# Attention by seven products: the fifth product's two sums move from ScalarE and GpSimd to VectorE

## The chip, the core and the metric

The kernel runs on one core of a Trainium2 chip. The metric is the device time of one launch in microseconds. Five compute queues run side by side and meet only at semaphores: TensorE (PE in the profile, its weight loads PEld), VectorE (DVE), ScalarE (ACT), GpSimd (POOL), and SyncE (SP), which issues DMAs. The granted TensorE clock is 1.00 of full speed over the whole profiled execution.

## The reference

The reference is a two-layer block on x of 64 x 32 x 512 in fp32: an S4D convolution, attention with 32 heads of width 128, a LoRA projection, an octonion feed-forward network, and a second layer of adapters, a small attention and a mixture of experts. Only the attention of the first layer bears on this change. Cut to what matters, with x of 2048 tokens x 512:

```python
q = x @ wq            # 512 -> 32 heads x 128
k, v = x @ wk, x @ wv
s = q @ k.T * 192 ** -0.5          # inside each batch of 32 tokens, causal
p = softmax(s)
x = x + (p @ v) @ wo               # summed over the 32 heads
```

## The kernel before

**Products.** Every projection is a product of a 2 x 2 block matrix of weights with a 2 x 2 block matrix of activations, and is made by seven products in place of eight (Winograd's form). A *set* is one such product: its seven results are P1 to P7, each 128 x 512 in one PSUM bank, and four outputs are sums of them:

- u2 = P6 + P1
- first output: P2 + P1
- u3 = P7 + u2
- second output: P4 + u3
- third output: u3 + P5
- u2 = u2 + P5, and then the fourth output: P3 + u2

Each fp32 product is made from a high and a low part of both operands by three matmuls (`mm3`, L215 to L217). So a product is 6 matmuls of 512 columns, or in the sets for the values (V) 12 of 256 columns.

**Loops.** `attention` runs 16 iterations: 8 groups of four heads (QUADS) for the first half of the tokens (pair 0), then 8 for the second (pair 1). Iterations 1 to 6 and 9 to 14 are hardware loops; 0, 7, 8 and 15 are written out. An iteration has six sets: 0 and 1 (weights H0, H1), 2 and 3 (values, weights V), 4 and 5 (H2, H3). After sets 0, 1, 4 and 5 come `scores` (16 matmuls of Q with K), a softmax on VectorE (`soft_shift`, `exps` on ScalarE, `soft_divide`, `soft_turn`), `prob_times_v`, and four `output` products with their `add_out`. In pair 0 VectorE also makes the activations' sums for the second half (`part`), which ScalarE stores to HBM by DMA.

**Who frees the banks.** The products use PSUM banks 0 to 2 in rotation (`product_bank`), in the order in which TensorE makes them: P1 of a set (ahead of P4 and P3 of the set before), P6, P5, P2, P7, the next P1, P4, P3. So a product waits until the one three places earlier has been read. Readers before the change: ScalarE copies P1 (`keep_p1`, L1230) and P5 (`keep_p5`, L1237) to SBUF; VectorE's `mix` (L1374, its addition is L1387) reads P6, P2, P7, P4 and P3 from PSUM with one operand in SBUF; GpSimd's `mix` (L1177) adds the copy of P5 to u3 (L1181) and to u2 (L1182). `mix_done` counts VectorE's sums, 5 a set, and `c22_done` GpSimd's.

**Weights.** SyncE loads them to `raw`. For every kind (H0, H1, V, H2, H3) ScalarE makes seven high parts (`high`, L973) and GpSimd seven low parts (`low`, L1007) and four sums of blocks (`sums`, L986, L989, L992, L996). A slot is overwritten once the product that used it is done: `sums` starts when product number 2 (P5) of the set that uses the slots is done, and the high part j waits for product j. A product waits for its own low part by the count in `lo_done`; the parts are made in the order 0 to 6, which is P1, P6, P5, P2, P7, P4, P3.

**Order.** Each queue's order is written out by hand in its `body`. `scores` of a set waits until P3's sum of that set is done, since it reads Q and K, and for the softmax step before (`soft_step`).

Of the kernel before, what the change touches and what calls it, by code (L numbers as in the profile page):

```python
# [14 lines left out]
F32 = mybir.dt.float32  # L15
# [881 lines left out]
PROD_AT = (1, 4, 5, 6, 7, 9, 10)  # L897
# [142 lines left out]
def attention(nc, t, sb, sem, overlaid, const, consts, mm3, resid, psum, kept_raw, kept, hw, v_tok, combos, later):  # L1040
# [7 lines left out]
    with ctx:  # L1048
# [4 lines left out]
        p5 = kept_raw[:, 7 * 2 * VCOLS + TT:7 * 2 * VCOLS + 2 * TT]  # L1053
# [15 lines left out]
        p1_done, p5_done = sem(ctx, "p1_done"), sem(ctx, "p5_done")  # L1069
        mix_done, c22_done = sem(ctx, "mix_done"), sem(ctx, "c22_done")  # L1070
# [56 lines left out]
        def _(sp):  # L1127
# [6 lines left out]
            def load_y(it, j):  # L1134
                sp.wait_ge(prod_done, product_count(it * SETS + SETS - 1, j))
                sp.wait_ge(part_out, 16 * (it * 7 + PART_ORDER.index(j) + 1))
                if j >= 2:
                    sp.wait_ge(y_in[j % 2], 16 * (j // 2))
                sp.dma_start(yc[:, j].bitcast(F32), y_parts[j]).then_inc(y_in[j % 2], 16)
# [31 lines left out]
        def _(pool):  # L1171
# [5 lines left out]
            def mix(it, s):  # L1177
                g = it * SETS + s
                pool.wait_ge(p5_done, g + 1)
                pool.wait_ge(mix_done, mix_count(g, 2))  # L1180
                pool.tensor_tensor(destination(s, 1, 1), u3[:], p5, ALU.add).then_inc(c22_done, 1)  # L1181
                pool.tensor_tensor(u2[:], u2[:], p5, ALU.add).then_inc(c22_done, 1)  # L1182

            def body(it, pair, first=False, turn=False, turned=False, last=False):
                hw.first_low(pool, it, "H1")
                mix(it, 0)
# [4 lines left out]
                mix(it, 1)  # L1191
                hw.last_low(pool, it, "V", fresh=first)
                hw.first_low(pool, it, "H2")
                mix(it, 2)
                hw.last_low(pool, it, "H2")
                mix(it, 3)
                out_low(it * 2 + 1)
                hw.first_low(pool, it, "H3")
                mix(it, 4)
# [3 lines left out]
                mix(it, 5)  # L1203
# [21 lines left out]
        def _(act):  # L1225
# [4 lines left out]
            def keep_p1(it, s):  # L1230
                g = it * SETS + s
                act.wait_ge(prod_done, product_count(g, 0))
                act.wait_ge(mix_done, g * 5 + 2)
                act.activation(p1, psum[:, product_bank(s, 0), :], ACT.Copy).then_inc(p1_done, 1)  # L1234

            def keep_p5(it, s, first=False):
                g = it * SETS + s  # L1237
                act.wait_ge(prod_done, product_count(g, 2))
                if not (first and s == 0):
                    act.wait_ge(c22_done, g * 2)  # L1240
                act.activation(p5, psum[:, product_bank(s, 2), :], ACT.Copy).then_inc(p5_done, 1)  # L1241
# [23 lines left out]
            def body(it, pair, first=False, turn=False, turned=False, last=False):  # L1265
# [6 lines left out]
                keep_p5(it, 0, first)  # L1272
# [9 lines left out]
                keep_p5(it, 1)  # L1282
# [10 lines left out]
                keep_p5(it, 2)  # L1293
# [6 lines left out]
                keep_p5(it, 3)  # L1300
# [5 lines left out]
                keep_p5(it, 4)  # L1306
# [11 lines left out]
                keep_p5(it, 5)  # L1318
# [29 lines left out]
        def _(dve):  # L1348
# [25 lines left out]
            def mix(it, s, k):  # L1374
                g = it * SETS + s
                j = (1, 3, 4, 5, 6)[k]
                dve.wait_ge(prod_done, product_count(g, j))
                out, other = ((u2[:], p1), (destination(s, 0, 0), p1), (u3[:], u2[:]),
                              (destination(s, 1, 0), u3[:]), (destination(s, 0, 1), u2[:]))[k]
                if k == 0:  # L1380
                    dve.wait_ge(p1_done, g + 1)
                    dve.wait_ge(mix_done, g * 5 + 5)
                if k in (2, 3):
                    dve.wait_ge(mix_done, mix_count(g, 0 if k == 2 else 2))
                if k == 4:
                    dve.wait_ge(c22_done, g * 2 + 2)
                dve.tensor_tensor(out, psum[:, product_bank(s, j), :], other, ALU.add).then_inc(mix_done, 1)  # L1387
# [51 lines left out]
            def body(it, pair, first=False, turn=False, turned=False, last=False):  # L1439
# [1552 lines left out]
```

## Time and profile before

| | us |
|---|---|
| median of 3 runs | 2131.43 (2130.31 to 2131.95) |
| profiled execution, its own time | 2132.61 |
| its span | 2130.8 |
| PE busy | 2101.4 (99%), 11928 matmuls |
| DVE busy | 1387.7 (65%) |
| POOL busy | 1248.8 (59%) |
| ACT busy | 718.4 (34%) |

The attention lies from about 89 to 1613 us of the span. Its loop iterations take about 94.5 us each. A matmul of 512 columns shows 390 ns, but the next one starts 0.23 us after it: they are pipelined and their ends are modelled. So a wait of TensorE shows as idle time only by what it exceeds that overlap. In the rows, kept_f is the memory that holds the copies of P1 and P5, wh and kept hold the weights, yc the activations, u is u2 or u3, sc and ex are the softmax's, probT the turned probabilities, v_tok and qk the outputs of the sets.

### The profile page before, as it was taken

What the parts mean: (1) busy time and instruction counts of PE and PEld (TensorE: products, weight loads), DVE (VectorE), ACT (ScalarE), POOL (GpSimd) and SP (SyncE); (2) the same over time, 40 slices, a digit from 0 to 9 for tenths busy, and PEclk for the clock granted to TensorE, in tenths of its full rate; (3) what the DMA queues carried; (4) which work ended last, traced back from release to release, by engine and by line L of the source; (5) the groups of instructions that cost most, each with busy time, mean ns of one, the idle gap of its engine ahead of it and who ended that gap; (6) DMA issues with size and microseconds to landing.
All of it is one profiled execution on the core that took longest, in us unless ns stands there. A gap on an engine that the chain in (4) does not pass through costs nothing. (4 is left out here: it accounts for less than half of the span.)

```text
span 2130.8 us, 36899 instructions
## 1 busy us (share of the span) xinstructions
PE 2101.4 (99%) x11928; PEld 1820.1 (85%) x11928; DVE 1387.7 (65%) x2625; ACT 718.4 (34%) x1444; POOL 1248.8 (59%) x1309
## 2 busy tenths in 40 slices
PE   7999999999999999999999999999999999999999
PEld 6788888989888898989888898989887788878887
DVE  8767777676767767665656566565657766655444
ACT  5333232332323232332323233232323744443332
POOL 3678585777757676776758576776745642114220
PEclk9999999999999999999999999999999999999999
DMA  7421212211111226211111211111112200001110
GB/s 241 154 60 48 55 49 79 54 52 47 49 52 44 75 58 215 61 41 41 40 39 42 67 49 39 39 39 39 40 61 77 90 20 0 0 1 40 39 39 20
DMA packets 122615, 122.28 MB, mean 57 GB/s; under 512 B 35249, under 2 KB 101457, under 8 KB 120497
## 3 DMA queue, kind: packets, MB, share of 16 engines
q1 hardware_dynamic: 91697, 109.87, 16.6%
q10 hardware_dynamic: 29568, 7.34, 1.7%
q0 software_dynamic: 1280, 4.20, 0.7%
q8 instruction: 37, 0.61, 0.1%
q14 instruction: 33, 0.27, 0.0%
HBM read 108.13 MB, written 13.28 MB: 57 GB/s over the span
## 5 line engine op out<-in xcount | busy, mean ns | idle before, releaser
L215 PE MATMUL psum<-yc,wh 128*128 128x512 f32 x904 | 361.4, 400 | 1.4 <-ACT kept_f L1234 0.8
L216 PE MATMUL psum<-yc,wh 128*128 128x512 f32 x904 | 352.9, 390 | 0.0
L217 PE MATMUL psum<-yc,wh 128*128 128x512 f32 x904 | 352.8, 390 | 0.0
L1437 DVE TENSOR_TENSOR resid<-psum,resid 128x512 f32<-128x512 f32 x248 | 171.3, 691 | 138.1 <-PE psum L217 133.8
L215 PE MATMUL psum<-kept,yc 128*128 128x256 f32 x896 | 256.7, 287 | 3.4 <-DVE u L1387 1.6
L217 PE MATMUL psum<-kept,yc 128*128 128x256 f32 x896 | 253.9, 283 | 0.0
L216 PE MATMUL psum<-kept,yc 128*128 128x256 f32 x896 | 253.8, 283 | 0.0
L1007 POOL TENSOR_TENSOR wh<-wh_f,wh 128x256 fp32r<-128x256 f32 x256 | 189.2, 750 | 105.1 <-ACT wh L973 102.9
L1007 POOL TENSOR_TENSOR wh<-raw,wh 128x256 fp32r<-128x256 f32 x192 | 142.0, 740 | 111.7 <-ACT wh L973 111.7
L217 PEld LDWEIGHTS psum<-yc,wh 128*128 128x128 f32 x904 | 169.8, 188 | 36.0
L215 PEld LDWEIGHTS psum<-yc,wh 128*128 128x128 f32 x904 | 170.4, 188 | 33.5 <-issue 1.4
L216 PEld LDWEIGHTS psum<-yc,wh 128*128 128x128 f32 x904 | 170.3, 188 | 30.8
L215 PE MATMUL psum<-o_hi,wo 128*128 128x512 f32 x496 | 194.4, 392 | 0.9 <-DVE resid L1437 0.9
L216 PE MATMUL psum<-o_lo,wo 128*128 128x512 f32 x496 | 194.2, 391 | 0.0
L217 PE MATMUL psum<-o_hi,wo 128*128 128x512 f32 x496 | 193.2, 390 | 0.0
L215 PEld LDWEIGHTS psum<-kept,yc 128*128 128x128 f32 x896 | 171.5, 191 | 8.8 <-DVE u L1387 2.5
L216 PEld LDWEIGHTS psum<-kept,yc 128*128 128x128 f32 x896 | 171.7, 192 | 3.6
L217 PEld LDWEIGHTS psum<-kept,yc 128*128 128x128 f32 x896 | 171.6, 192 | 0.0
L973 ACT ACTIVATE wh<-wh_f 128x256 fp32r<-128x256 f32 x256 | 98.4, 408 | 176.8 <-POOL wh_f L996 158.9
L1241 ACT ACTIVATE kept_f<-psum 128x512 f32<-128x512 f32 x96 | 57.4, 598 | 263.0 <-PE psum L217 263.0
L1234 ACT ACTIVATE kept_f<-psum 128x512 f32<-128x512 f32 x96 | 57.1, 595 | 220.8 <-PE psum L217 204.4
L1387 DVE TENSOR_TENSOR u<-psum,kept_f 128x512 f32<-128x512 f32 x96 | 66.4, 692 | 94.9 <-PE psum L217 93.8
(363 smaller groups left out, 4925.3 us busy)
## 6 DMA issues: line engine op xcount, KB each, us to landing
raw<-in_attn_w SPq DMA_DIRECT2D x96, 512.0 KB, 5.1
wo_f<-in_attn_w SPq DMA_DIRECT2D x31, 512.0 KB, 4.0
hankel<-kernel_rows SPq DMA_DIRECT2D x32, 256.0 KB, 4.6
y_parts<-stage ACTq DMA_DIRECT2D x56, 128.0 KB, 2.3
yc<-y_parts SPq DMA_DIRECT2D x7, 1024.0 KB, 5.1
resid<-in_xT SPq DMA_DIRECT2D x4, 1024.0 KB, 9.7
outT<-wide SPq DMA_DIRECT2D x16, 256.0 KB, 2.6
kept_f<-in_l_w SPq DMA_DIRECT2D x3, 1024.0 KB, 5.5
```

Of the source, the lines that this page charges most:

```text
L215: pe.matmul(out, w[0], x[0], start=start, stop=False)
L216: pe.matmul(out, w[0], x[1], start=False, stop=False)
L217: return pe.matmul(out, w[1], x[0], start=False, stop=stop)
L973: act.activation(self.part(kind, j, 0), src, ACT.Copy).then_inc(self.hi_done, 1)
L1007: pool.tensor_tensor(self.part(kind, j, 1), src, self.part(kind, j, 0).bitcast(F32), ALU.subtract).then_inc(self.lo_done, 1)
L1234: act.activation(p1, psum[:, product_bank(s, 0), :], ACT.Copy).then_inc(p1_done, 1)
L1241: act.activation(p5, psum[:, product_bank(s, 2), :], ACT.Copy).then_inc(p5_done, 1)
L1387: dve.tensor_tensor(out, psum[:, product_bank(s, j), :], other, ALU.add).then_inc(mix_done, 1)
L1437: dve.tensor_tensor(part, psum[:, 5 + (GH + m) % 3, :], part, ALU.add).then_inc(tail_free, 1)
```

## The change

In place of the copy on ScalarE and the two sums on GpSimd, VectorE's `mix` reads P5 from PSUM twice: third output = P5 + u3, then u2 = P5 + u2. That is seven VectorE sums a set, all counted by `mix_done`. `keep_p5`, GpSimd's `mix`, the buffer p5 and the semaphores p5_done and c22_done are gone. TensorE makes P7 ahead of P5: P6, P7, P5, P2, the next P1, P4, P3, and the banks follow. `mix` takes the sums in the order P6, P7, P5 to the third output, P5 to u2, P2, P4, P3. The order of the low and high parts of the weights and the numbers of the products are unchanged (P5 is still number 2, P7 number 4). The places of `scores`, `prob_times_v`, `output`, `add_out`, `part` and the softmax steps are set anew around the sums. The activations that pair 1 loads back come in the new order (Y_ORDER). `keep_p1` now waits for P2's sum of the set before.

```diff
-PROD_AT = (1, 4, 5, 6, 7, 9, 10)
+PROD_AT = (1, 4, 6, 7, 5, 9, 10)
 def product_bank(s, j):
-    return (s * 7 + (-3, 0, 1, 2, 3, 5, 6)[j]) % 3
+    return (s * 7 + (-3, 0, 2, 3, 1, 5, 6)[j]) % 3
 def mix_count(g, k):
-    return g * 5 + (6 + k)
+    return g * 7 + (8 + k)
...
-            def mix(it, s):
-                g = it * SETS + s
-                pool.wait_ge(p5_done, g + 1)
-                pool.wait_ge(mix_done, mix_count(g, 2))
-                pool.tensor_tensor(destination(s, 1, 1), u3[:], p5, ALU.add).then_inc(c22_done, 1)
-                pool.tensor_tensor(u2[:], u2[:], p5, ALU.add).then_inc(c22_done, 1)
...
-                act.wait_ge(mix_done, g * 5 + 2)
+                act.wait_ge(mix_done, mix_count(g, 4) - 7)
                 act.activation(p1, psum[:, product_bank(s, 0), :], ACT.Copy).then_inc(p1_done, 1)
-            def keep_p5(it, s, first=False):
-                ...
-                act.activation(p5, psum[:, product_bank(s, 2), :], ACT.Copy).then_inc(p5_done, 1)
...
+            def mix(it, s, *ks):
                 g = it * SETS + s
+                for k in ks:
+                    name = ("P6", "P7", "P5", "P5", "P2", "P4", "P3")[k]
+                    out, other = ((u2[:], p1), (u3[:], u2[:]), (destination(s, 1, 1), u3[:]), (u2[:], u2[:]),
+                                  (destination(s, 0, 0), p1), (destination(s, 1, 0), u3[:]), (destination(s, 0, 1), u2[:]))[k]
+                    dve.wait_ge(prod_done, product_count(g, PROD[name]))
+                    if k == 0:
+                        dve.wait_ge(p1_done, g + 1)
+                        dve.wait_ge(mix_done, mix_count(g, 6) - 7)
+                    elif k in (1, 2, 6):
+                        dve.wait_ge(mix_done, mix_count(g, {1: 0, 2: 1, 6: 3}[k]))
+                    dve.tensor_tensor(out, psum[:, product_bank(s, PROD[name]), :], other, ALU.add).then_inc(mix_done, 1)
...
                 if not first:
                     soft_shift(sm)
-                mix(it, 0, 1)
+                mix(it, 0, 1, 2, 3, 4)
                 if not first:
                     soft_divide(sm)
-                mix(it, 0, 2)
-                if not first:
                     soft_turn(sm, 1, it * 8)
-                mix(it, 0, 3)
-                mix(it, 0, 4)
+                mix(it, 0, 5, 6)
...
                 elif name != "P1":
-                    pe.wait_ge(mix_done, {"P5": g * 5 + 4, "P2": g * 5 + 5, "P7": mix_count(g, 0),
-                                          "P4": mix_count(g, 1), "P3": mix_count(g, 2)}[name])
+                    pe.wait_ge(mix_done, {"P7": mix_count(g, 5) - 7, "P5": mix_count(g, 6) - 7, "P2": mix_count(g, 0),
+                                          "P4": mix_count(g, 3), "P3": mix_count(g, 4)}[name])
                 elif not start:
-                    pe.wait_ge(p5_done, g)
+                    pe.wait_ge(mix_done, mix_count(g, 1) - 7)
...
                 pe.wait_ge(soft_step, sm * NSOFT - 4)
-                pe.wait_ge(mix_done, mix_count(g, 4))
+                pe.wait_ge(mix_done, mix_count(g, 6))
```

The first place is VectorE in set 0 of an iteration, from the last step of `soft_shift` to the P3 sum of the set (kept_f32 is P1's copy; here a written-out iteration). Before:

```order
L1410 TENSOR_TENSOR sc<-sc,stat 128x256
L1387 TENSOR_TENSOR qk<-psum,kept_f32 128x512
L1417 TENSOR_REDUCE stat<-ex 128x8
L1418 RECIPROCAL stat<-stat 128x8
L1419 TENSOR_TENSOR ex<-ex,stat 128x256
L1387 TENSOR_TENSOR u3<-psum,u2 128x512
L1425 STREAM_TRANSPOSE probT<-ex 32x8x32 x4
L1387 TENSOR_TENSOR qk<-psum,u3 128x512
L1387 TENSOR_TENSOR qk<-psum,u2 128x512
```

The same stretch now:

```order
L1383 TENSOR_TENSOR sc<-sc,stat 128x256
L1360 TENSOR_TENSOR u3<-psum,u2 128x512
L1360 TENSOR_TENSOR qk<-psum,u3 128x512
L1360 TENSOR_TENSOR u2<-psum,u2 128x512
L1360 TENSOR_TENSOR qk<-psum,kept_f32 128x512
L1390 TENSOR_REDUCE stat<-ex 128x8
L1391 RECIPROCAL stat<-stat 128x8
L1392 TENSOR_TENSOR ex<-ex,stat 128x256
L1398 STREAM_TRANSPOSE probT<-ex 32x8x32 x4
L1360 TENSOR_TENSOR qk<-psum,u3 128x512
L1360 TENSOR_TENSOR qk<-psum,u2 128x512
```

Four sums stand together ahead of the division, where one stood; the transposes and the last two sums follow it, with nothing between the division and the transposes.

The second place is GpSimd while TensorE is in set 0: the low parts of H1 (wh), in a hardware loop, with the register work for the waits. Before:

```order
L1007 TENSOR_TENSOR wh<-wh_f32,wh 128x256
L1179 REGISTER_ALU
L1180 ISA
L1181 TENSOR_TENSOR qk<-u3,kept_f32 128x512
L1182 TENSOR_TENSOR u2<-u2,kept_f32 128x512
L1004 REGISTER_ALU
L1007 TENSOR_TENSOR wh<-raw,wh 128x256
```

The same stretch now:

```order
L1007 TENSOR_TENSOR wh<-wh_f32,wh 128x256
L1004 REGISTER_ALU
L1007 TENSOR_TENSOR wh<-raw,wh 128x256
L995 REGISTER_ALU
L996 TENSOR_TENSOR wh_f32<-raw 128x256
```

The two sums with the copy of P5 are gone, and the next low part follows the last at once.

## Rows read from the trace of the kernel before

**Rows 1.** The page: the engines' busy time, us and share of the span.

```profile
PE 2101.4 (99%) x11928; PEld 1820.1 (85%) x11928; DVE 1387.7 (65%) x2625; ACT 718.4 (34%) x1444; POOL 1248.8 (59%) x1309
```

**Rows 2.** TensorE's waits, 90 to 140 us: waited for, total, times, longest.

```profile
PE psum L215 <- ACT kept_f L1234: 1.3, 2, 0.8
PE psum L215 <- DVE v_tok L1387: 1.0, 1, 1.0
...
PE psum L1682 <- DVE qk L1387: 0.5, 1, 0.5
```

**Rows 3.** The same view, 140 to 1580 us.

```profile
PE psum L215 <- DVE u L1387: 1.4, 1, 1.4
```

**Rows 4.** Groups of instructions: busy us, mean ns, idle before.

```profile
L1182 POOL TENSOR_TENSOR u<-u,kept_f 128x512 f32<-128x512 f32 x96 | 124.4, 1296 | 0.0
```

**Rows 5.** Timeline of TensorE, set 0 of iteration 4: start us, us.

```profile
462.56 0.39 PE L215 MATMUL psum<-yc,wh 128*128 128x512 f32 x1
...
463.92 0.39 PE L215 MATMUL psum<-yc,wh 128*128 128x512 f32 x1
...
470.73 1.95 PE L1682 MATMUL psum<-qk 128*128 128x128 f32 x16
```

**Rows 6.** Timeline of VectorE, the same set, and set 1's shift.

```profile
458.54 0.68 DVE L1387 TENSOR_TENSOR qk<-psum,u 128x512 f32<-128x512 f32 x1
...
463.59 0.42 DVE L1410 TENSOR_TENSOR sc<-sc,stat 128x256 f32<-128x256 f32 x1
464.12 0.69 DVE L1387 TENSOR_TENSOR qk<-psum,kept_f 128x512 f32<-128x512 f32 x1
464.73 0.41 DVE L1417 TENSOR_REDUCE stat<-ex 128x8 f32<-128x256 f32 x1
...
465.41 0.42 DVE L1419 TENSOR_TENSOR ex<-ex,stat 128x256 f32<-128x256 f32 x1
466.05 0.69 DVE L1387 TENSOR_TENSOR u<-psum,u 128x512 f32<-128x512 f32 x1 [0.21 <-DVE ex L1419]
466.66 1.77 DVE L1425 STREAM_TRANSPOSE probT<-ex 32x256 f32<-32x256 f32 x4
468.46 0.69 DVE L1387 TENSOR_TENSOR qk<-psum,u 128x512 f32<-128x512 f32 x1
469.66 0.69 DVE L1387 TENSOR_TENSOR qk<-psum,u 128x512 f32<-128x512 f32 x1 [0.51 <-POOL u L1182]
...
474.92 1.34 DVE L1410 TENSOR_TENSOR sc<-sc,stat 128x256 f32<-128x256 f32 x1
```

**Rows 7.** Timeline of GpSimd, the same stretch.

```profile
462.80 0.73 POOL L986 TENSOR_TENSOR wh_f<-raw 128x256 f32<-128x256 f32 x1 [3.18 <-PE psum L217]
463.62 1.00 POOL L989 TENSOR_TENSOR wh_f<-wh_f,raw 128x256 f32<-128x256 f32 x1
...
473.62 2.37 POOL L1174 TENSOR_TENSOR wo<-wo_f,wo 128x1024 fp32r<-128x1024 f32 x1
```

**Rows 8.** Timeline of VectorE, set 2: steps after shift and division.

```profile
498.91 0.42 DVE L1410 TENSOR_TENSOR sc<-sc,stat 128x256 f32<-128x256 f32 x1
499.37 0.69 DVE L1437 TENSOR_TENSOR resid<-psum,resid 128x512 f32<-128x512 f32 x1
...
501.25 0.71 DVE L1419 TENSOR_TENSOR ex<-ex,stat 128x256 f32<-128x256 f32 x1
502.09 0.69 DVE L1437 TENSOR_TENSOR resid<-psum,resid 128x512 f32<-128x512 f32 x1
```

**Rows 9.** Timeline of VectorE, the last set (iteration 15).

```profile
1583.55 0.42 DVE L1410 TENSOR_TENSOR sc<-sc,stat 128x256 f32<-128x256 f32 x1
...
1589.30 0.69 DVE L1387 TENSOR_TENSOR qk<-psum,u 128x512 f32<-128x512 f32 x1 [0.38 <-POOL u L1182]
```

**Rows 10.** Timeline of TensorE: the scores after that set.

```profile
1590.14 0.57 PE L1811 MATMUL psum<-qk 128*128 128x128 f32 x3
```

**Rows 11.** Timeline of GpSimd, iteration 0: the fifth low part of V.

```profile
118.98 1.29 POOL L1007 TENSOR_TENSOR kept<-kept_f,kept 128x512 fp32r<-128x512 f32 x1 [0.74 <-ACT kept L973]
```

More of the change, by code:

```diff
@@ L1490, in body @@
                     add_out(T + 1, 1, before, 1)
+                mix(it, 2, 4)
+                if not first:
                     add_out(T + 1, 2, before, 1)
-                mix(it, 2, 3)
+                mix(it, 2, 5)
                 if not first:
                     add_out(T + 1, 3, before, 1)
-                mix(it, 2, 4)
+                mix(it, 2, 6)
                 part(4)
@@ L1524, in body @@
                 soft_shift(sm + 3)
+                mix(it, 5, 1)
                 if not last:
                     add_out(T + 3, 0, pair, 1)
-                mix(it, 5, 1)
-                soft_divide(sm + 3)
+                mix(it, 5, 2, 3)
                 if not last:
                     add_out(T + 3, 1, pair, 1)
-                mix(it, 5, 2)
+                soft_divide(sm + 3)
+                mix(it, 5, 4)
+                if not last:
+                    add_out(T + 3, 2, pair, 1)
                 part(6)
                 if not last:
-                    add_out(T + 3, 2, pair, 1)
                     add_out(T + 3, 3, pair, 1)
                 soft_turn(sm + 3, 0, it * 8 + 8)
-                mix(it, 5, 3)
-                mix(it, 5, 4)
-            dve.sem_inc(mix_done, 5)
+                mix(it, 5, 5, 6)
+            dve.sem_inc(mix_done, 7)
             dve.sem_inc(soft_step, NSOFT)
@@ L1714, in body @@
                     scores(sm, it * SETS - 1)
+                product(it, 0, "P7", fresh=fresh)
                 product(it, 0, "P5", fresh=fresh)
                 product(it, 0, "P2", fresh=fresh)
-                product(it, 0, "P7", fresh=fresh)
                 product(it, 1, "P1")
@@ L1723, in body @@
                 scores(sm + 1, it * SETS)
[L1724 removed]
+                product(it, 1, "P7")
                 if not first:
                     prob_times_v(T, 1, 0, sm + 1, it * SETS - 3)
+                product(it, 1, "P5")
                 product(it, 1, "P2")
[L1728 removed]
                 product(it, 2, "P1")
@@ L1741, in body @@
                 product(it, 2, "P6")
+                product(it, 2, "P7")
+                scores(sm + 2, it * SETS + 1)
                 product(it, 2, "P5")
-                scores(sm + 2, it * SETS + 1)
-                product(it, 2, "P2")
                 if not first:
                     output(T + 1, 0, it * 2)
-                product(it, 2, "P7")
+                product(it, 2, "P2")
                 if not first:
@@ L1758, in body @@
                 product(it, 3, "P6")
+                product(it, 3, "P7")
                 product(it, 3, "P5")
                 product(it, 3, "P2")
-                product(it, 3, "P7")
                 product(it, 4, "P1")
@@ L1781, in body @@
                 scores(sm + 3, it * SETS + 4)
+                product(it, 5, "P7")
+                if not last:
+                    output(T + 3, 0, it * 2 + 1)
                 product(it, 5, "P5")
                 if not last:
-                    output(T + 3, 0, it * 2 + 1)
+                    output(T + 3, 1, it * 2 + 1)
                 product(it, 5, "P2")
-                if not last:
-                    output(T + 3, 1, it * 2 + 1)
-                product(it, 5, "P7")
                 if not last:
```

82 lines of the change are left out of this document (25 added, 57 removed).

## The prediction, made before the change had run

> **What bounds the kernel now.** I read the page first: TensorE is busy 99% of the span, VectorE 65%, GpSimd 59%, ScalarE 34% [rows 1]. So work taken from ScalarE and GpSimd, or put on VectorE, costs or gives only what TensorE waits for it. The view of waits says what that is. In iteration 0 of the attention TensorE stands idle for banks and weights about 3 us, in five or six places [rows 2]; in the whole stretch from 140 to 1580 us the view has one wait, 1.4 us for u [rows 3]. Idle time here is what exceeds the overlap of two matmuls: a matmul shows 0.39 us and starts 0.23 us after the last, so each wait costs 0.16 us more than it shows. All waits of these two stretches together are therefore worth some 5 us (3.3 + 1.4 and 0.16 for each). That is the most that the change could save there, 0.25% of the time. What it can lose is any new wait that comes back in each of 15 iterations. So the timeline of one iteration decides, and I read it with the queues' new order beside it.
>
> **The work itself.** Gone are 96 copies on ScalarE and 192 sums on GpSimd, near 1.3 us each [rows 4], about 250 us; new are 96 more sums on VectorE at 0.69 us [rows 6], 66 us (seven in a set for five, less the wait for GpSimd). None of it is on TensorE. The sums read PSUM and one operand in SBUF and took 0.69 us each, whatever GpSimd did.
>
> **Banks.** TensorE may start a product when the sum of the one three places before is done, two products of 1.36 us later. P5 now has two sums, 0.61 us apart (464.12 to 464.73, the spacing of a PSUM sum and what follows [rows 6]). Laid out below for set 0, the densest, P7's sum ends at 464.74 and the next P1 starts at 465.28; P5's second sum ends at 466.07 and P4 starts at 466.64. Half a microsecond is left at both. In sets 1, 2, 4 and 5 scores and output products lie between, and more is left; in set 3 as much. I charge nothing for banks; the cover is that half microsecond.
>
> **Scores after set 0.** This is the term that decides. Before: the last sum (469.66) ended at 470.35, TensorE started the scores at 470.73 [rows 5, 6]. At the end of the attention a sum ends at 1589.99 and the scores that waited for it start at 1590.14 [rows 9, 10]: 0.15 us behind. So the last sum has to end by 470.58; 0.23 us were spare. Now, in iteration 4:
> - The shift's last step ends at 463.59 + 0.42 = 464.01. The next operation comes 0.04 later (499.33 to 499.37 [rows 8]): P7's sum 464.05 to 464.74. P7 is done long before, since it is made where P5 was.
> - P5's first sum needs u3: 464.77 to 465.46. P5 is then done, as P2 starts at 463.92 [rows 5]. Second sum 465.38, P2's sum 465.99.
> - The division starts 0.61 later, 466.60; its last step 0.68 later (464.73 to 465.41), 467.28, and takes 0.42: 467.70.
> - The transposes follow 0.13 later, the gap between a division in a hardware loop and the next operation (501.96 to 502.09 [rows 8]): 467.83, and 1.77 us: 469.60.
> - P4's sum comes 0.03 later (468.43 to 468.46): 469.63. P3's 0.61 later: 470.24 to 470.93. The scores start at 471.08, 0.35 us late.
>
> Before, the division and the transposes lay in VectorE's waits for products; now two sums more stand ahead of them and the four steps behind run without a gap. Everything behind the scores on TensorE is late by as much, in each iteration from 1 to 15: 15 x 0.35 = 5.2. In the three written-out iterations the 0.13 should be shorter, so I take 5.0. Bounds: nothing, if the steps run 0.35 us tighter than I have put them, and 0.6 an iteration, 9 us, if every gap is as long as the longest (0.21 behind the division [rows 6]).
>
> **The last set.** Iteration 15 has the same chain with no products behind it. From 1583.97 (the shift's end [rows 9]): sums at 1584.01, 1584.73, 1585.34, division 1585.95, its last step 1586.63 to 1587.05, P2's sum 1587.09 (here it stands behind the division), transposes 1587.70, P4's sum 1589.50, P3's 1590.11 to 1590.80, scores 1590.95 for 1590.14: +0.8. There VectorE sets the pace, so it stays. Before, the last sum waited 0.38 for GpSimd [rows 9]; that wait goes, but the two sums more outweigh it.
>
> **Iteration 0.** Of the waits [rows 2] the second of ScalarE's two (0.5), v_tok's 1.0, qk's 0.5 and some smaller ones that the view lists go, since they were waits for GpSimd's sums or for the queue behind them; with 0.16 each, about 3.7. But P7 now needs the fifth low part as the second product of a set. For V in iteration 0 that part was started at 118.98 [rows 11]. GpSimd loses four sums ahead of it, 5.2 us, but starts the sums of H1 1.4 us later (they wait for P5), so it may come by 115.2 and be done at 116.5; TensorE would get to P7 of set 2 at 114.5. Price 2.0, between 0 (115.2 less all that is uncertain) and 5. P1 behind the shift of set 1 loses 0.4, P3 of set 2 0.3. Net: -0.9, from -3 to +2. In later iterations GpSimd is ahead: for H1 the fifth low part is done by 471.0 and P7 of set 1 starts at 472.4; for V it is ready some 3.5 us early.
>
> **The wait of 1.4 us** [rows 3] is in iteration 5, where part 3 stood on VectorE ahead of P7's sum and waited for a store. It now stands behind P2's sum; what is late next is ScalarE's copy of the next P1, which stands behind the store of part 3, by about 1. With two short waits of the same place: -0.9, from 0 to -2.
>
> **The sum**: 5.0 + 0.8 - 0.9 - 0.9 = +4.0 us. The profiled execution took 2132.61 for a span of 2130.8, 1.2 above the median of 2131.43; the difference goes onto the median: 2135.4.
>
> **Rivals.**
> 1. *GpSimd takes the memory port at the division* (slower for certain). VectorE's steps with two SBUF operands wait for a running GpSimd operation: set 1's shift step took 1.34 us for 0.42, and ended at 476.26, 0.27 after GpSimd's (473.62 + 2.37 = 475.99) [rows 6, 7]. In set 0 GpSimd's first sum now starts 0.24 after P5 is done, as before (462.56 to 462.80 [rows 5, 7]): 464.16, three sums 0.82 apart, the low part of P6 at about 466.61 to 467.35, the next at 467.31. The division's last step comes at 467.28. Ahead of the next low part by 0.03 it takes its 0.42; behind it, it ends 0.27 after that, at 468.32, 0.62 later. It decides from a shift of 0.03 us on. Price 15 x 0.62 = 9.3, time 2144.7. For it: the margin is less than my error. Against: an operation that already waits when GpSimd's ends is served first. The Trainium skill says of this port (SBUF — State Buffer, section "SBUF: two separate sides") that whichever starts first holds it for the whole instruction; by that rule the 0.03 us decides between 2135.4 and 2144.7.
> 2. *The steps run tighter and no scores wait*: 0.8 - 1.8 = -1.0, 2130.4. For it: 0.35 us is made of eight small gaps. Against: each was read in this trace.
> 3. *The waits go and nothing replaces them*, the low parts of V included: -5 at most, 2126.4, faster. Against: the chain above has no slack for it.
> 4. *GpSimd is not relieved where it counts, since its sums of weights start later*: if the fifth low part of H1 came 1.4 us later than I have it (the slack at P7 of set 1), TensorE would wait in each iteration; at 0.3 each, 4.5 more, 2139.9. It stands at the end of a chain across three engines.
>
> **How the numbers follow.** Forecast 0.56, rival 1 0.18, rival 2 0.14, rival 3 0.04, rival 4 0.08. About 0.2%, 4.3 us, is what a measurement of this kernel can tell from no change: 2127.2 to 2135.7. The forecast's own range is 2133.0 to 2138.0; its value lies just inside the bound, so it gives 0.30 to same and 0.25 to slower, and 0.01 to faster. Rival 2 goes to same, rivals 1 and 4 to slower, rival 3 to faster. That makes same 0.44, slower 0.51, faster 0.05. The range must reach to rival 2 and to rival 1: 2130.0 to 2144.5.
>
> **What would show it.** Right: TensorE waits in 15 places at the first scores of set 1 (qk released by VectorE), with an iteration of 94.7 to 95.0 us for 94.55; no wait for banks in set 0; the division's last step in set 0 at 0.42 us; the wait in iteration 5 shorter; in iteration 0 a wait at P7 of set 2 for a low part of kept. A division step of 1.0 us in set 0 is rival 1; scores of set 1 without a wait is rival 2; a wait of P7 for wh is rival 4. The forecast is wrong if TensorE's waits in a loop iteration add up to under 0.1 or over 0.6 us.

## The result

| | median us | range, runs | ratio to the kernel before, 95% interval |
|---|---|---|---|
| kernel before (same session) | 2132.12 | 2130.31 to 2134.45, 12 | 1 |
| changed kernel | 2136.46 | 2134.79 to 2141.71, 12 | 1.0021, 1.0013 to 1.0028 |

The changed kernel is slower by 4.3 us by the medians and 4.5 by the ratio, where +4.0 was forecast; below, +4.4 stands for both. The interval leaves out 1, so the loss is small but clear of the noise. Its profiled execution took 2141.71 us, the longest of its twelve, for a span of 2139.9. So 9.1 us of span lie between the two traces, and only about half of it belongs to the change, as the split below shows.

### The profile page after: what moved, and what is told of

The parts are those of the page before. It is cut to its first block and busy times, and to the rows that moved or that the text cites. A ratio compares the mean times of both kernels' runs of the same rounds, so it can differ in the third digit from the quotient of the medians.

```text
span 2139.9 us, 36441 instructions
## 1 busy us (share of the span) xinstructions
PE 2109.2 (99%) x11928; PEld 1822.2 (85%) x11928; DVE 1479.3 (69%) x2817; ACT 667.1 (31%) x1348; POOL 1012.2 (47%) x1117
## 5 line engine op out<-in xcount | busy, mean ns | idle before, releaser
L986 POOL TENSOR_TENSOR wh_f<-raw 128x256 f32<-128x256 f32 x64 | 47.5, 742 | 244.8 <-PE psum L217 244.8
L1360 DVE TENSOR_TENSOR qk<-psum,u 128x512 f32<-128x512 f32 x192 | 129.6, 688 | 47.2 <-PE psum L217 42.5
L1360 DVE TENSOR_TENSOR u<-psum,u 128x512 f32<-128x512 f32 x192 | 131.5, 685 | 9.6 <-PE psum L217 7.1
```

Source lines behind the costliest of these rows:

```text
L986: pool.tensor_tensor(s1, a21, a22, ALU.add).then_inc(self.sum_done, 1)
L1360: dve.tensor_tensor(out, psum[:, product_bank(s, PROD[name]), :], other, ALU.add).then_inc(mix_done, 1)
```

## The profile after

The page's busy lines, which answer to [rows 1]:

```profile
PE 2109.2 (99%) x11928; PEld 1822.2 (85%) x11928; DVE 1479.3 (69%) x2817; ACT 667.1 (31%) x1348; POOL 1012.2 (47%) x1117
```

GpSimd lost 237 us of work and ScalarE 51; VectorE has 192 more sums and is busy for 92 us more. TensorE has the same 11928 matmuls. None of this tells what happened to the time.

TensorE's waits from 85 to 1620 us of the changed kernel (total, times, longest), which answer to [rows 2, 3]:

```profile
PE psum L215 <- POOL kept L1007: 1.9, 1, 1.9
PE psum L215 <- DVE u L1360: 1.4, 2, 0.9
...
PE psum L215 <- ACT kept_f L1221: 1.0, 2, 0.8
...
PE psum L1654 <- DVE qk L1360: 0.5, 3, 0.2
```

The last line is the forecast wait, scores (L1654) for VectorE's last sum into qk. The view counts three of them with 0.5 us and would make the reader pass on. But each of the 15 iterations has one. In the hardware loops it shows only 0.055 to 0.07 us, under what the view lists; the three that it lists are those of the written-out iterations 7, 8 and 15.

VectorE in set 0 of iteration 4 of the changed kernel (start, duration), which answers to [rows 6]:

```profile
468.10 0.42 DVE L1383 TENSOR_TENSOR sc<-sc,stat 128x256 f32<-128x256 f32 x1
468.55 0.69 DVE L1360 TENSOR_TENSOR u<-psum,u 128x512 f32<-128x512 f32 x1
469.28 0.69 DVE L1360 TENSOR_TENSOR qk<-psum,u 128x512 f32<-128x512 f32 x1
469.89 0.68 DVE L1360 TENSOR_TENSOR u<-psum,u 128x512 f32<-128x512 f32 x1
470.48 0.68 DVE L1360 TENSOR_TENSOR qk<-psum,kept_f 128x512 f32<-128x512 f32 x1
471.08 0.41 DVE L1390 TENSOR_REDUCE stat<-ex 128x8 f32<-128x256 f32 x1
...
471.76 0.42 DVE L1392 TENSOR_TENSOR ex<-ex,stat 128x256 f32<-128x256 f32 x1
472.31 1.79 DVE L1398 STREAM_TRANSPOSE probT<-ex 32x256 f32<-32x256 f32 x4
474.13 1.29 DVE L1360 TENSOR_TENSOR qk<-psum,u 128x512 f32<-128x512 f32 x2
```

From the shift's end (468.52) to the end of the last sum (475.42) there is no idle row: 6.90 us. The working of the prediction had 6.92 for it (464.01 to 470.93).

TensorE's scores of the same iteration, the ones ahead of that chain and the ones behind it:

```profile
463.90 1.95 PE L1654 MATMUL psum<-qk 128*128 128x128 f32 x16
475.47 2.05 PE L1654 MATMUL psum<-qk 128*128 128x128 f32 x16
```

The scores come 0.05 us behind the last sum, not 0.15 as I had put it: 0.15 was read in a written-out iteration, and in iterations 7, 8 and 15 of the changed kernel it is 0.15 again. But the same 16 matmuls last 0.10 us longer than those that did not wait. Measured against the kernel before, where 6.72 us lay between the shift's end and the scores (464.01 to 470.73 [rows 5, 6]), it is 6.95 now, +0.23, and 0.1 in the block itself. Together that is nearly all of what the iteration gained: from one set 1's scores to the next it took 94.54 us before (1040.18 to 1134.72) and 94.90 now (1046.04 to 1140.94), +0.36.

GpSimd in the same stretch, which answers to [rows 7]:

```profile
468.70 0.74 POOL L986 TENSOR_TENSOR wh_f<-raw 128x256 f32<-128x256 f32 x1 [4.69 <-PE psum L217]
...
471.16 1.62 POOL L1007 TENSOR_TENSOR wh<-wh_f,wh 128x256 fp32r<-128x256 f32 x2
```

Its first low part ends at about 471.90 (471.16 + 0.74) and the second starts about 472.04 (472.78 less 0.74). The division's last step (471.76 to 472.18) came ahead of the second, and the end of the first, 0.28 us before its own, did not hold it up: it took its 0.42 us.

The split of the 9.1 us between the two profiled executions, by the starts of the same instructions:

| stretch | after less before, us | of it the change |
|---|---|---|
| up to the first scores | +2.5 | 0 |
| iteration 0, from there | +0.8 | -0.7, the rest is 1.6 of half clock |
| iterations 1 to 14 | +4.1 | 14 x 0.36 = 5.0; -0.9 of other waits, see below |
| iteration 15 up to the last set | +0.4 | +0.4 |
| last set | +0.9 | +0.9 |
| after the attention | +0.4 | 0 |

The -0.7 of iteration 0 is read from the traces of runs 1 and 5, whose iteration 0 is the changed kernel's and ran at the full clock: 72.1 us, for 72.8 before and 73.7 in the changed kernel's own trace. The third column gives 4.7, and medians and ratio 4.3 to 4.5. The stretch ahead of the attention, before and after (us, busy time of PE, PEld, DVE, ACT and POOL, then the granted clock, DMA share and GB/s), of the kernel before and of the changed one:

```profile
50.00:89.00 39.00, 35.32 (x247) 31.38 (x246) 32.12 (x56) 14.44 (x29) 20.81 (x23) 1.00 0.58 185
```

```profile
50.00:91.00 41.00, 37.61 (x245) 33.45 (x245) 31.41 (x55) 14.14 (x29) 20.34 (x22) 0.92 0.54 174
```

Code that the change does not touch ran at a mean granted clock of 0.92 there in this one execution. That is not the change's.

## The experiments

All were compared with the kernel before on the same chip. There were three groups of runs (1 to 4, 5 to 7, 8 to 10 below), each on another chip, and the medians of the kernel before were 2132.48, 2130.61 and 2131.64 us in them. So across groups the ratios are the fair comparison.

| run | median us | ratio to before, 95% | loop iteration us |
|---|---|---|---|
| 1 turn_behind | 2129.94 | 0.9989, 0.9980 to 0.9998 | 94.54 |
| 2 parts_in_order | 2140.07 | 1.0035, 1.0021 to 1.0049 | 95.47 |
| 3 both | 2126.52 | 0.9971, 0.9959 to 0.9983 | 94.54 |
| 4 before_turn_behind | 2131.93 | 0.9997, 0.9988 to 1.0006 | 94.54 |
| 5 third_sum | 2144.69 | 1.0065, 1.0051 to 1.0078 | 95.59 |
| 6 order_alone | 2202.66 | 1.0338, 1.0324 to 1.0352 | 97.6 to 101.5 |
| 7 copy_first | 2125.43 | 0.9976, 0.9967 to 0.9985 | 94.54 |
| 8 sum_between | 2134.91 | 1.0012, 1.0003 to 1.0021 | 94.90 |
| 9 sums_alone | 2145.85 | 1.0069, 1.0055 to 1.0082 | 95.4 to 97.2 |
| 10 sums_alone_turn_behind | 2146.08 | 1.0066, 1.0052 to 1.0080 | 95.4 to 97.4 |

An iteration here goes from its first block of scores to that of the next; where one number stands, it is that of most iterations.

### 1. The transposes behind the last two sums of set 0

```diff
                 if not first:
                     soft_divide(sm)
-                    soft_turn(sm, 1, it * 8)
                 mix(it, 0, 5, 6)
+                if not first:
+                    soft_turn(sm, 1, it * 8)
```

> The changed kernel, with set 0's transposes (the softmax of the tile before) put behind the P4 and P3 sums of set 0, in place of ahead of them. Theory A (the chain in front of the next set's scores is what the change lengthened: two more VectorE sums ahead of the division): the P3 sum comes about 0.5 us sooner, the scores no longer wait, each of 15 iterations falls from 94.90 to about 94.55, and the kernel is 5.0 to 5.5 us faster than the changed kernel, about 2131, the time of the kernel before. The product of probabilities and values, the transposes' reader, has more than 3 us in hand. Theory B (the cost is iteration 0's new wait for GpSimd's low parts, with the fall of the granted clock behind it): no change, 2136. Theory C (VectorE's 92 us of added work slow it everywhere through the port it shares with GpSimd): no change, or under 1 us.

Measured: 2129.94, 0.9989 of the kernel before, where the changed kernel stood at 1.0021: 6.8 us less by the ratios, for the expected 5.0 to 5.5; the two intervals leave some 2.5 us either way. VectorE and TensorE in set 0 of iteration 4:

```profile
465.32 0.69 DVE L1360 TENSOR_TENSOR qk<-psum,u 128x512 f32<-128x512 f32 x1 [0.62 <-PE psum L217]
466.69 0.69 DVE L1360 TENSOR_TENSOR qk<-psum,u 128x512 f32<-128x512 f32 x1 [0.68 <-PE psum L217]
467.30 1.77 DVE L1398 STREAM_TRANSPOSE probT<-ex 32x256 f32<-32x256 f32 x4
```

```profile
467.54 0.39 PE L217 MATMUL psum<-yc,wh 128*128 128x512 f32 x1
467.77 1.95 PE L1655 MATMUL psum<-qk 128*128 128x128 f32 x16
```

VectorE now waits for TensorE (0.62 and 0.68 us), the last sum ends at 467.38, the scores follow their predecessor by the ordinary 0.23 us and take 1.95. The iteration is 94.54, as in the kernel before. Theory A holds: iterations 1 to 14 lost 6.1 us between the two traces. Of these 5.0 are the scores. The other 1.1 is mostly ScalarE's copy of P1, which was late in iterations 3, 4 and 5 of the changed kernel's trace (0.26, 0.43 and 0.28 us) and hardly here. The edit alone doesn't remove it: run 3, which has the edit too, shows the late copy again (iterations 4 and 5 of 94.82 and 95.07 us). Theories B and C expected nothing here and fall as the main cause.

### 2. The weights' parts in the order of the products

```diff
+PARTS = (0, 1, 4, 2, 3, 5, 6)
...
         self.low(pool, it, kind, (0,))
-        self.sums(pool, it, kind, (0, 1, 2), fresh)
-        self.low(pool, it, kind, (1, 2))
+        self.sums(pool, it, kind, (0, 1, 2, 3), fresh)
+        self.low(pool, it, kind, (1, 4))
...
-        self.low(pool, it, kind, (3,))
-        self.sums(pool, it, kind, (3,), fresh)
-        self.low(pool, it, kind, (4, 5, 6))
+        self.low(pool, it, kind, (2, 3, 5, 6))
```

ScalarE's high parts follow the same order, (1, 4, 2) and (3, 5, 6) in place of (1, 2, 3) and (4, 5, 6).

> The changed kernel, with the weights' high and low parts and their third sum made in the order in which the products now run (P1, P6, P7, P5, P2, P4, P3; GpSimd's sum for P7 moved ahead of the second low part). Theory A: iteration 0's P7 of set 2 no longer waits its 2.0 us; the late scores stay; 2.0 us faster than the changed kernel, 3.7 if the 3.4 us at half clock go with the wait, so 2132.5 to 2134.5. Theory B: this is most of the +4.4 us: 2132. Theory C: no change. Against all: P5's part now comes two low parts later, so a wait of up to 1 us can turn up at P5 or P2 of set 2 in iteration 0.

Measured: 2140.07, so 3.6 us slower than the changed kernel (3.0 by the ratios), where each theory had it faster or the same. All missed. The wait in iteration 0 is gone as expected, but the loops pay. TensorE's waits, 140 to 1580 us:

```profile
PE psum L1653 <- DVE qk L1359: 9.6, 15, 0.7
```

Now the 15 late scores stand in the view, at 0.64 us each. That is idle time as shown; from the start of the matmul ahead to the start of the scores it is 1.02 us, 0.79 over the ordinary 0.23, where the changed kernel has 0.22 over it. The difference is the 0.57 by which the iteration grew. VectorE and GpSimd in set 0 of iteration 4:

```profile
463.91 1.00 DVE L1391 TENSOR_TENSOR ex<-ex,stat 128x256 f32<-128x256 f32 x1
465.04 1.79 DVE L1397 STREAM_TRANSPOSE probT<-ex 32x256 f32<-32x256 f32 x4
```

```profile
460.85 0.74 POOL L987 TENSOR_TENSOR wh_f<-raw 128x256 f32<-128x256 f32 x1 [4.68 <-PE psum L217]
...
462.49 0.74 POOL L993 TENSOR_TENSOR wh_f<-raw,wh_f 128x256 f32<-128x256 f32 x1
463.19 0.74 POOL L997 TENSOR_TENSOR wh_f<-raw 128x256 f32<-128x256 f32 x1
463.88 2.33 POOL L1008 TENSOR_TENSOR wh<-wh_f,wh 128x256 fp32r<-128x256 f32 x3
```

This is rival 1 of the prediction, brought about by an edit that had nothing to do with VectorE. GpSimd's fourth sum depends on no operation just before it and starts 0.70 us behind its predecessor, where a dependent one starts 0.82 behind (461.67 to 462.49). GpSimd's fifth operation, the low part of P6, then starts 3.03 us after its first, 0.03 ahead of the division's last step (463.91, 3.06 after it). That step took 1.00 us in place of 0.42 and ended at 464.91, 0.29 behind GpSimd's operation (464.62). In the changed kernel GpSimd's fifth operation was due 0.70 behind the fourth, at 471.86, the step had come 0.10 before that (471.76), and it was GpSimd's operation that started late. 0.57 us an iteration hang on it (95.47 less 94.90).

### 3. Both edits

> The changed kernel with both edits: set 0's transposes behind the last two sums, and the weights' parts made in the order of the products. Theory A: the gains add: 5.2 + 2.0 to 3.7 = 7 to 9 us faster than the changed kernel, 2127.5 to 2129.5, so 3 to 4.5 us faster than the kernel before. Theory B: as the run with the parts in order alone, about 2132. Theory C: 2136.

Measured: 2126.52, 0.9971 of the kernel before: 6.2 us faster than it by the ratio, 9.9 less than the changed kernel by the medians, somewhat more than the 7 to 9 expected. The division's last step is as long as in run 2, but with the transposes behind the last sums the scores don't feel it: 94.54. From the first block of scores in iteration 0 to the first in iteration 1 it takes 69.0 us, for 72.1 in run 1: gone are the wait for P7's low part (1.9 shown) and one for P1's bank (0.5 shown), and what each costs beyond what it shows.

### 4. The kernel before with the transposes behind

The same edit as in run 1, in the kernel before.

> The kernel before, with set 0's transposes put behind its P3 sum. Theory A: nothing waits at the scores in the kernel before, so there is nothing to gain: 2132.1, within 0.2%. If the kernel before gains 4 us or more too, the transposes' place is worth something of its own and its gain in the changed kernel does not show that the two added sums were the cost.

Measured: 2131.93, 0.9997 (0.9988 to 1.0006). No difference, as theory A has it. What the edit gives in the changed kernel undoes something that the change brought. The trace shows one thing more: the wait of 1.4 us for u in iteration 5 of the kernel before [rows 3] is here 0.2 us in iteration 5 and 0.2 in iteration 6, though the edit is elsewhere. So its size is not fixed by the order of the queues alone.

### 5. A third sum in the chain

```diff
-                mix(it, 0, 1, 2, 3, 4)
+                mix(it, 0, 1, 2, 3)
+                if not first:
+                    spare_sum(it)
+                mix(it, 0, 4)
```

> The changed kernel with one more VectorE sum in set 0 of the 15 iterations, of the same shape (P2's bank plus the kept P1, 128x512, written to a buffer that nothing reads), ahead of P2's own sum. Theory A (each sum ahead of the scores' last operand now costs its full pitch, 0.60 us by the starts 469.28, 469.89 and 470.48 of the three sums in a row): 15 x 0.60 = +9 us on the changed kernel, 2145.5; the transposes' first-come lock with GpSimd can move this by 0.3 us an iteration either way (2141 to 2150). Theory C (what counts is VectorE's busy time as such, 92 us for +4.4 us): 15 x 0.69 = 10 us of work would bring under 0.5 us, 2137.

Measured: 2144.69, forecast 2145.5; by the ratios 9.4 us more than the changed kernel. The iteration is 95.59, +0.69 for the expected 0.60. The rest stands in the rows, VectorE and GpSimd:

```profile
468.27 0.51 DVE L1397 TENSOR_TENSOR ex<-ex,stat 128x256 f32<-128x256 f32 x1
468.91 1.79 DVE L1403 STREAM_TRANSPOSE probT<-ex 32x256 f32<-32x256 f32 x4
```

```profile
467.07 1.43 POOL L1007 TENSOR_TENSOR wh<-wh_f,wh 128x256 fp32r<-128x256 f32 x2
```

GpSimd's second low part ended at 468.50, and the division's step at 468.78, 0.28 behind it: 0.51 in place of 0.42. So 0.60 for the sum and 0.09 for the port. The forecast had put such a delay down to the transposes; but each of them took 0.42 to 0.44 us throughout the attention, beside GpSimd's operations or not, here and in the two kernels. VectorE's own work grew by 10 us and the time by 9.4. The 92 us of work that the change adds cost nothing where they don't stand in the chain: in run 1, which has them too, the iteration is the old 94.54 (theory C falls). What counts is where a sum stands.

### 6. The order alone

The changed kernel's order of products and sums, with P5 copied by ScalarE and added by GpSimd as before. P4 takes P5's bank, so it waits for ScalarE's copy:

```diff
+                    if name == "P4":
+                        pe.wait_ge(p5_done, g + 1)
...
+            def mix(it, s):
+                g = it * SETS + s
+                pool.wait_ge(p5_done, g + 1)
+                pool.wait_ge(mix_done, mix_count(g, 1))
+                pool.tensor_tensor(destination(s, 1, 1), u3[:], p5, ALU.add).then_inc(c22_done, 1)
+                pool.tensor_tensor(u2[:], u2[:], p5, ALU.add).then_inc(c22_done, 1)
```

> The order of the products and of VectorE's sums as in the changed kernel (P7 ahead of P5), but P5 still copied by ScalarE and added by GpSimd, as in the kernel before. Theory A: in front of set 0's P3 sum VectorE has no sum more than in the kernel before, so iterations 1 to 14 stay at 94.55 and the scores don't wait; iteration 0 keeps the waits that GpSimd's additions bring and gets P7's, so +1 to +4 there: 2133 to 2136 in all, by another cause than the changed kernel's. Rival D (the order is what costs, not the added sums): late scores in 15 places, 94.8 to 94.95 an iteration. A mixture is possible: GpSimd's two additions now can start ahead of the division's last step (its P7 sum comes earlier) and hold it up by up to 1.4 us, in which case that step lasts over 0.42 us in the trace.

Measured: 2202.66, 1.0338 of the kernel before, +71 us. I had expected no change in the loops; they take 97.6 us at best and 101.5 at worst. VectorE and GpSimd in set 0 of iteration 4:

```profile
493.59 0.69 DVE L1393 TENSOR_TENSOR qk<-psum,u 128x512 f32<-128x512 f32 x1
494.77 0.69 DVE L1393 TENSOR_TENSOR qk<-psum,u 128x512 f32<-128x512 f32 x1 [0.49 <-POOL u L1184]
```

```profile
492.20 1.28 POOL L1183 TENSOR_TENSOR qk<-u,kept_f 128x512 f32<-128x512 f32 x1
493.45 1.29 POOL L1184 TENSOR_TENSOR u<-u,kept_f 128x512 f32<-128x512 f32 x1
```

The last sum waits for GpSimd's sum of u, and TensorE's scores for it (0.64 us shown). The waits of 140 to 1580 us show that this is the smaller part:

```profile
PE psum L215 <- DVE o_lo L1437: 17.6, 24, 1.3
PE psum L215 <- ACT kept_f L1236: 12.8, 7, 1.9
PE psum L1690 <- DVE qk L1393: 9.4, 14, 0.9
```

P5 is made one product later, and with it ScalarE's copy, GpSimd's two sums and all that is queued behind them. Iteration 0 adds 6.3 us, with one wait of 6.4 for a low part of V. And the mean granted clock was 0.995 or 0.996 in all five executions, for 0.999 or 1.000 in those of the kernel before: by an estimate from that, some 9 us (0.004 of 2201) of the 71 are clock. So the order without the moved sums is a bad kernel, and its late scores have another cause than the changed kernel's. Rival D's 94.8 to 94.95 did not come, but neither did theory A's 94.55: this run doesn't decide between them. Runs 5 and 9 do.

### 7. ScalarE's copy ahead of the store

```diff
-                store(3)
                 keep_p1(it, 4)
+                store(3)
```

This is run 3 with ScalarE's copy of P1 of set 4 ahead of the store of part 3.

> The version with both edits (transposes behind, parts in the products' order), with ScalarE's copy of P1 of set 4 put ahead of the store of part 3. It stands behind that store now, and P1's copy was late in iterations 3 to 7 by 0.5 to 1.0 us in all. Theory A: these waits go, 0.5 us, up to 1 us: 2125.5 to 2126.5, no difference that the measurement can tell from the version with both edits; against the kernel before 0.997, faster.

Measured: 2125.43, 0.9976 (0.9967 to 0.9985), not to be told from run 3 (0.9971). In the trace the waits are gone: iterations 1 to 14 lie between 94.51 and 94.56, where run 3 had 94.82 and 95.07 in iterations 4 and 5. It and run 3 are the versions that beat both kernels.

### 8. GpSimd's sum moved back by one place

Run 2 with one line's order changed:

```diff
-        self.sums(pool, it, kind, (0, 1, 2, 3), fresh)
-        self.low(pool, it, kind, (1, 4))
+        self.sums(pool, it, kind, (0, 1, 2), fresh)
+        self.low(pool, it, kind, (1,))
+        self.sums(pool, it, kind, (3,), fresh)
+        self.low(pool, it, kind, (4,))
```

> The kernel with the parts in the products' order (no other edit), with GpSimd's sum for P7 moved back by one place, between the low parts of P6 and P7. In the run with the parts in order the scores were 0.64 us late in place of 0.22, and the division's last step took 1.00 us where it takes 0.42 in the changed kernel: GpSimd's low part of P6 began at 463.88, 0.03 us ahead of that step (463.91), and ended at 464.62. Theory P (a step of VectorE that reads two SBUF operands waits for the GpSimd operation that runs when it comes up, and ends 0.27 to 0.29 us behind it): with one operation less in front, GpSimd's low part of P6 starts about 2.46 us behind its first sum and ends 3.20 behind it, so the step (3.06 behind it) ends no later than it would anyway: 0.42 to 0.45 us, iterations of 94.9 in place of 95.47, 15 x 0.57 = 8.5 us less, 2131 to 2132. Rival Q (the order of ScalarE's copies, or the later parts of P5 and P2, made the iterations longer): 95.4, 2140.

Measured: 2134.91, 5.2 us less than run 2 by the medians. The loop iteration is back at 94.90. VectorE and GpSimd:

```profile
467.98 0.42 DVE L1393 TENSOR_TENSOR ex<-ex,stat 128x256 f32<-128x256 f32 x1
```

```profile
464.91 0.75 POOL L987 TENSOR_TENSOR wh_f<-raw 128x256 f32<-128x256 f32 x1 [4.46 <-PE psum L217]
...
467.37 0.73 POOL L1008 TENSOR_TENSOR wh<-wh_f,wh 128x256 fp32r<-128x256 f32 x1
468.06 0.94 POOL L997 TENSOR_TENSOR wh_f<-raw 128x256 f32<-128x256 f32 x1
```

The low part starts 2.46 us after the first sum, as expected, and ends ahead of 468.12 (468.40 less 0.28); the division's step takes 0.42, and GpSimd's next operation, 0.08 us behind it, is the one that lasts longer (0.94 for 0.74). Theory P holds for the step, and Q falls: the high parts' order is the same in both runs. The Trainium skill (SBUF — State Buffer, section "SBUF: two separate sides") says that of two such operations the one that starts first has the shared port for its whole instruction; runs 2 and 8 agree, with the step at 1.00 and 0.42 us. GpSimd's operation started 0.03 us ahead of the step in run 2, and the next one 0.08 behind it in run 8. TensorE's wait is not the changed kernel's, though its iteration has the same length. In run 8 no scores start late: in all 15 iterations they follow the matmul ahead by 0.23 or 0.24 us. TensorE waits six matmuls earlier, at P6 of set 1, for ScalarE's copy of P1:

```profile
469.66 0.58 ACT L1222 ACTIVATE kept_f<-psum 128x512 f32<-128x512 f32 x1
```

```profile
470.30 0.50 PE L215 MATMUL psum<-yc,wh 128*128 128x512 f32 x1
```

The copy stands behind the high part for P7, and that waits for the very sum that was moved back (468.06 to 469.00). VectorE's chain from the shift to the last sum still takes 6.91 us, as in the changed kernel, so its delay is hidden in this wait and would show without it.

In all I expected 8.5 us and got 5.2 (4.9 by the ratios). Iterations 1 to 14 took 7.7 us less (1337.5 and 1329.8); 1.3 us came back in iteration 0, whose waits are 0.1 us for a low part, 0.1 for u, 0.4 for a copy of P1 and 0.3 for v_tok, and the profiled execution's stretch ahead of the attention was longer too. What of this is in the medians I can't separate.

### 9 and 10. The sums alone, in the old order of the products

All seven sums on VectorE, with P5 + u2 kept in the buffer p5 and P7's bank read twice:

```diff
+                for k in ((0,), (1, 2), (3, 4), (5,), (6,))[step]:
+                    name = ("P6", "P5", "P2", "P7", "P7", "P4", "P3")[k]
+                    out, other = ((u2[:], p1), (p5, u2[:]), (destination(s, 0, 0), p1), (u3[:], u2[:]),
+                                  (destination(s, 1, 1), p5), (destination(s, 1, 0), u3[:]), (destination(s, 0, 1), p5))[k]
```

> All sums of a product set on VectorE, as in the changed kernel, but the products in the order of the kernel before (P1, P6, P5, P2, P7, P4, P3): P5's bank is read once (P5 + u2, kept in the buffer of the former copy) and P7's bank twice. No copy by ScalarE, no additions by GpSimd; seven VectorE sums a set. Theory A (two more sums in front of the scores' operand): late scores in 15 places, iterations 94.8 to 95.0, or 95.5 if the division's last step now falls on a GpSimd operation; iteration 0 without the 3.7 us of waits that GpSimd's additions brought and without the 2.0 us for P7's part, which is needed two products later: 2131 + 5 + 1 - 4.6 = 2132.5, or 2141 with the collision. Rival D (the products' order is what costs): iterations 94.55, 2127.5.

> The same with set 0's transposes behind its last two sums. Theory A: the late scores go whatever the division's step does, iterations 94.54: 2127, the time of the version with both edits within 0.1%. Rival D: no different from the sums alone.

Measured: 2145.85 and 2146.08, +14 us in both. The first lies beyond the two cases I had given, and the second, with the transposes behind, gained nothing, where I expected 2127. TensorE's waits of 140 to 1580 us, run 9 and then run 10:

```profile
PE psum L215 <- DVE kept_f L1359: 4.5, 15, 0.4
PE psum L215 <- DVE v_tok L1359: 4.2, 6, 1.6
```

```profile
PE psum L215 <- DVE kept_f L1359: 8.7, 15, 0.7
PE psum L215 <- DVE v_tok L1359: 3.6, 6, 1.8
```

The first wait, in all 15 iterations, is another one: for the bank of P5, whose sum writes the kept buffer. The second, for a sum of set 2 or 3, comes once in each of iterations 1 to 6, and the changed kernel has it only in iteration 0 (0.3 us); no run shows its cause. VectorE in set 1 of iteration 1, run 9:

```profile
189.38 1.29 DVE L1403 TENSOR_TENSOR o_lo<-psum,o_hi 128x512 fp32r<-128x512 f32 x2 [0.97 <-ACT o_hi L1229]
190.59 0.68 DVE L1359 TENSOR_TENSOR kept_f<-psum,u 128x512 f32<-128x512 f32 x1
```

and TensorE's next product, P1 of set 2:

```profile
191.32 0.39 PE L215 MATMUL psum<-kept,yc 128*128 128x256 f32 x1 [0.29 <-DVE kept_f L1359]
```

In the old order P1 of the next set takes P5's bank, and P5's sum stands behind `o_low`. In the changed kernel P1 waits for P7's sum, which stands ahead of `o_low`. So each half of the change, as built here, costs more alone (+14 and +71 us) than the two together (+4.4). That the order of the products makes the difference is argued, not shown: P5 is the second product of a set in the old order as P7 is in the new, and no run put its sum ahead of `o_low` in the old order. Moving the transposes removed the late scores (0.12 to 0.21 us over a matmul's ordinary 0.23 in all 15 iterations of run 9, none in run 10), but pushed the softmax of set 1 and P5's sum back instead: the wait for it rose from 4.5 to 8.7 us. Rival D, which had iterations of 94.55 and 2127.5 for run 9, falls here: the scores are late with the sums alone, in the old order.

## Why the prediction was right, step by step

- **The work itself.** Miscounted, without effect on the sum: seven sums for five in 96 sets are 192 more on VectorE, not 96. Their durations add up to 131 us, not 66; VectorE's busy time grew by 92.
- **Banks: nothing.** Held. In set 0 of the changed kernel TensorE has no wait ahead of the scores, and 0.6 us were left at both banks (469.24 to 469.82, 470.57 to 471.18). Runs 9 and 10 show that this is not so for every order of the sums.
- **Scores after set 0, +5.0.** Held: 15 x 0.36 = 5.4, of which 5.0 in iterations 1 to 14. The chain was 6.90 us for 6.92. The parts of the wait were off: it shows 0.1 less at its front and the block of scores behind it lasts 0.1 longer, which cancel; that they do is luck. Run 1 removes it, run 4 shows that it was not there before, run 5 adds 0.69 to it.
- **The last set, +0.8.** Held: +0.86.
- **Iteration 0, -0.9.** Held: -0.7 where the clock stayed up (the prediction's own terms, -3.7 + 2.0 + 0.4 + 0.3, give -1.0). The low part that P7 waits for ended at 119.40 and P7 started at 119.45, a wait of 1.88 shown and 2.0 in all, as forecast:

```profile
118.13 1.27 POOL L1007 TENSOR_TENSOR kept<-kept_f,kept 128x512 fp32r<-128x512 f32 x1 [0.74 <-ACT kept L973]
```

```profile
119.45 0.44 PE L215 MATMUL psum<-kept,yc 128*128 128x256 f32 x1 [1.88 <-POOL kept L1007]
```

- **The wait of 1.4 us, -0.9.** The two traces have it so, but it isn't shown to be the change's. The wait is gone from iteration 5, and ScalarE's copy behind the store of part 3 is what is late next, by 0.26, 0.43 and 0.28 us in iterations 3 to 5. All such waits of iterations 1 to 14 together went from 2.5 to 1.6 us. But run 4, the old kernel with an edit elsewhere, has 1.7, and runs 1 and 3 have 0.5 and 0.9. One trace of each kernel can't tell this term from the difference between executions, so that the sum of the small terms came out is in part luck.
- **Rival 1, the memory port.** It did not come about in set 0 of the changed kernel, and came about with a margin of 0.03 us the other way in run 2. The price was 0.57 us an iteration for the forecast 0.62. A chance of 0.18 for it was not too much. In the other sets the step did get longer, 0.83 to 0.93 us in the loops for 0.50 to 0.72 before, and no scores were late there: only set 0 has no slack. Its time, 2144.7, lies 0.2 above the stated range, which was meant to reach to it.
- **Rivals 2 to 4.** No set of scores after set 0 was on time (2); the low parts of V did replace a wait in iteration 0 (3); P7 of set 1 never waited for wh in the loops (4).
- **The signs.** The iteration (94.90), the step of 0.42 us, the 15 places and the waits in iterations 0 and 5 came as stated. The last sign, waits under 0.1 us in a loop iteration, would have called the forecast wrong by what the profile shows as idle (0.055 to 0.07). It holds only if a wait is counted from start to start, 0.22 over the ordinary 0.23, and the prediction didn't say which it meant.

## What to carry to other kernels

An instruction that an engine has time for in the mean still costs its whole pitch where it stands in a chain that another engine waits for: follow the chain to the operand that is needed first, and put what is needed later (here the transposes, 1.8 us) behind it. This alone turned +4.4 us into -2.3, and with the producers of the weights' parts put in the order of their use into -6.2. A change of order and a change of engine that belong together can't be judged one at a time (the halves cost +71 and +14 us here), and a wait of 0.06 us in the trace can stand for 0.36 us an iteration: measure the iteration, not the idle time.

## What the runs showed of the hardware

- A VectorE step with two SBUF operands that comes up while a GpSimd operation runs ended 0.28 to 0.29 us behind it (468.50 to 468.78, 464.62 to 464.91). In the loops of five traces (both kernels, runs 2, 5 and 8) all shift and division steps of over 0.45 us, more than 300, ended so. VectorE's sums with one operand in PSUM took 0.68 or 0.69 us beside the same GpSimd operations.
- In the hardware loops, sixteen scores matmuls that had to wait for their operand lasted 2.05 us from the first start to the last end, and 1.95 us where they had not. The second starts 0.21 us behind the first in place of 0.11.
- Behind the 2 us wait in iteration 0 the changed kernel's execution ran at half the granted clock. Busy times of the engines in two stretches, then the clock:

```profile
117.00:119.50 2.50, 0.62 (x6) 0.42 (x5) 1.86 (x4) 1.97 (x4) 1.76 (x3) 1.00 0.00 0
119.50:123.00 3.50, 3.50 (x17) 3.50 (x18) 1.17 (x3) 0.00 (x0) 3.50 (x4) 0.52 0.00 0
```

The clock was at 1.00 (2.4 GHz) during the wait and at 0.52, nearly all at 1.2 GHz, for the 3.5 us behind it; that cost 1.6 us, by iteration 0 of runs 1 and 5. The executions of these two runs had the same wait and stayed at 1.00, so the fall is not bound to the wait alone (run 1):

```profile
114.00:118.00 4.00, 3.09 (x26) 3.09 (x27) 2.11 (x5) 0.86 (x3) 4.00 (x5) 1.00 0.00 0
```
